# Splitting the FFN weights into bf16 pairs ahead of attention instead of inside the first FFN token block

## What is computed

```python
x = layernorm(x + attn(x, Wq, Wkv_down, Wk_up, Wv_up, Wo))      # 8 heads of 256, kv latent of 64
x = layernorm(x + ffn(x, W1, b1, W2, b2, scale))
# ffn, with S = 2048, D = 1024, H = 4096; W1 [H, D], W2 [D, H]
h = x @ W1.T + scale * (x @ m1.T) + b1       # m1, m2: rank-4 matrices made from a few tokens of x
h = gelu(h)                                  # exact gelu
out = h @ W2.T + scale * (h @ m2.T) + b2
```

## Time and profile before

| | us |
|---|---|
| two timed executions | 4051.82 and 4417.59 (median 4234.71) |
| the profiled execution, time | 4072.83 |
| the profiled execution, span of its slowest core | 4071.2 |
| spans of the 8 cores in it | 4036.4 to 4071.2 |
| FFN token block 0 / 1 (from L915 to the next L915) | 870.7 / 448.4 |

### The profile page before, as it was taken

The page is one execution under the profiler, slowest core; times in us unless marked ns, Lnnn a source line. Parts: engine busy times, 40 slices in busy tenths (PEclk is TensorE's granted clock), DMA queues, the critical chain, the costliest instruction groups (busy, mean ns, idle before and its releaser), DMA issues.

```text
span 4071.2 us, 32532 instructions; the slowest of 8 cores (4036.4 to 4071.2 us)
## 1 busy us (share of the span) xinstructions
PE 3140.4 (77%) x10424; PEld 1208.2 (30%) x10610; DVE 743.4 (18%) x1123; ACT 506.0 (12%) x729; POOL 547.4 (13%) x1144
## 2 busy tenths in 40 slices
PE   3647769889889789626666566569998899978997
PEld 1512223323323233202222122213443334423442
DVE  1112221121121121131111000014201331023201
ACT  0000014234234134100000000001000110001000
POOL 0000000000000000016664555510000000000000
PEclk8578879999999999857778777789998899989998
DMA  3130000010010010026554445433233232323232
GB/s 111 62 109 0 0 27 6 4 43 6 4 44 6 3 46 6 7 75 115 105 114 77 88 94 100 95 79 96 66 98 100 76 86 72 96 63 88 66 97 64
DMA packets 474216, 253.89 MB, mean 62 GB/s; under 512 B 125170, under 2 KB 452850, under 8 KB 473026
## 3 DMA queue, kind: packets, MB, share of 16 engines
q1 hardware_dynamic: 315938, 177.63, 15.9%
q0 software_dynamic: 79776, 32.20, 5.7%
q10 hardware_dynamic: 78336, 41.98, 3.5%
HBM read 177.49 MB, written 50.33 MB: 56 GB/s over the span
## 4 chain that ended last, share of the span: by engine, by line
PE 63%; DMA 10%; POOL 10%; DVE 9%; issue 4%; ACT 2%; SPq 1%; DVEq 0%; POOLq 0%; ACTq 0%
PE psU L592 11%; DMA whl<-w2f 5%; PE ps L337 4%; PE psY L624 3%; DMA whl<-w1f 3%; PE ps L562 3%; POOL whl L751 3%; POOL whl L743 3%; PE ps L565 3%; PE ps L558 2%; POOL whl L789 2%; PE ps L1065 2%; PE ps L1070 2%; PE ps L1075 2%; PE psY L962 2%
## 5 line engine op out<-in xcount | busy, mean ns | idle before, releaser
L592 PE MATMUL psU<-et,kvtok 128*65 128x512 f32 x1024 | 523.1, 598 | 2.6
L578 ACT ACTIVATE et<-ps,Ubias 128x512 f32<-128x512 f32 x512 | 351.7, 687 | 643.9 <-PE psU L592 431.8
L995 ACT ACTIVATE hgf<-htmp,b1s 128x512 f32<-128x512 f32 x128 | 92.3, 721 | 1738.5 <-DVE htmp L989 1685.9
L1065 PE MATMUL psY<-hphi,whl 128*128 128x512 bf16 x504 | 209.7, 416 | 80.0 <-POOL whl L797 79.0
L1065 PE MATMUL ps<-hphi,whl 128*128 128x512 bf16 x500 | 207.1, 414 | 79.0 <-POOL whl L797 78.1
L962 PE MATMUL psY<-z1s,whl 128*128 128x512 bf16 x505 | 212.8, 421 | 61.1 <-POOL whl L751 49.1
L962 PE MATMUL ps<-z1s,whl 128*128 128x512 bf16 x496 | 202.9, 409 | 67.3 <-POOL whl L751 65.7
L967 PE MATMUL psY<-z1s,whl 128*128 128x512 bf16 x499 | 211.0, 423 | 10.2 <-POOL whl L751 5.9
L1070 PE MATMUL psY<-hplo,whl 128*128 128x512 bf16 x500 | 208.0, 416 | 11.2 <-POOL whl L797 10.6
L443 DVE RECIPROCAL rcp<-psU 1x512 f32<-1x512 f32 x32 | 107.4, 3355 | 573.3 <-PE psU L592 573.3
L1070 PE MATMUL ps<-hplo,whl 128*128 128x512 bf16 x504 | 209.2, 415 | 3.1 <-POOL whl L797 2.2
(11 more groups left out here) (172 smaller groups left out, 3146.9 us busy)
## 6 DMA issues: line engine op xcount, KB each, us to landing
whl<-w1sd SPq DMA_DIRECT2D x768, 64.0 KB, 1.9
whl<-w2sd SPq DMA_DIRECT2D x768, 64.0 KB, 1.9
w1f<-w1p SPq DMA_DIRECT2D x256, 64.0 KB, 3.5
w1sd<-whl ACTq DMA_DIRECT2D x256, 64.0 KB, 3.6
w2f<-w2p SPq DMA_DIRECT2D x256, 64.0 KB, 2.9
w2sd<-whl ACTq DMA_DIRECT2D x256, 64.0 KB, 3.0
xTs<-xT SPq DMA_DIRECT2D x8, 1024.0 KB
wst<-wq SPq DMA_DIRECT2D x16, 512.0 KB, 5.4
```

The lines of the kernel that those rows point to most:

```text
L578: P.op("scalar", lambda e, kc=kc, par=par, h=h: e.activation(out=et[:, par * 512:(par + 1) * 512], in_=psA[par][:], func=AF.Exp, bias=Ubia ...
L592: P.op("tensor", lambda e, kc=kc, par=par, h=h: e.matmul(psU[h % 2][:], kvtok[:, kc * 65:(kc + 1) * 65], et[:, par * 512:(par + 1) * 512], ...
L1065: P.op("tensor", lambda e, d=d, k=k, s4w=s4w, hc=hc, st=st: e.matmul(psP[d % 4][:], whl2[:, s4w * 1024 + k * 256: s4w * 1024 + k * 256 + 128],
```

## The change

The splitting leaves tb = 0. A new `plan_split_block()` handles the next of 96 blocks (W1's 32, then W2's 64) with two buffers of its own, wspf (float32) and wspb (split), which live until the end of attention: ScalarE issues the loads, GpSimd the casts and the subtractions, ScalarE the stores into w1sd and w2sd. Three blocks are planned after each of the 8 heads of the query folding, three after each of the 8 heads of the output folding, three after each of the 16 query tiles; that makes 96, all planned ahead of the U8 transfers of L369 in GpSimd's list. `plan_w1` and `plan_w2` in all token blocks are what tb >= 1 had: SP loads from w1sd and w2sd, four blocks ahead. They wait for all stores (SPL_T). The buffers w1f and w2f and the stores of tb = 0 go.

```diff
+        sSLD = [sems["sW2C0"], sems["sW2C1"]]
+        sSCA = [sems["sW1C0"], sems["sW1C1"]]
+        sSST = [sems["sST0"], sems["sST1"]]
+        split_blocks = ([("w1", hc) for hc in range(HCN)]
+                        + [("w2", gi) for gi in range(64)])
+        spl = {"i": 0, "sub": {}, "st": {}}
+
+        def plan_split_block():
+            if spl["i"] >= len(split_blocks):
+                return
+            kind, idx = split_blocks[spl["i"]]
+            sl = spl["i"] % 2
+            spl["i"] += 1
+            if kind == "w1":
+                nch = DC
+                src_ap = lambda c, idx=idx: w1p[idx, c * 128:(c + 1) * 128, :]
+                dst_ap = lambda c, idx=idx: w1sd[idx, c * 128:(c + 1) * 128, :]
+            else:
+                d, g = divmod(idx, 8)
+                nch = 4
+                src_ap = lambda c, d=d, g=g: w2p[d, (g * 4 + c) * 128:(g * 4 + c + 1) * 128, :]
+                dst_ap = lambda c, d=d, g=g: w2sd[d, (g * 4 + c) * 128:(g * 4 + c + 1) * 128, :]
+            for c in range(nch):
+                P.op("scalar", lambda e, c=c, sl=sl, src_ap=src_ap: e.dma_start(
+                    out=wspf[:, sl * 1024 + c * 128: sl * 1024 + (c + 1) * 128],
+                    in_=src_ap(c)),
+                    waits=[(cG, spl["sub"].get(sl, 0))], inc=sSLD[sl], inc_k=16)
+            vL = sSLD[sl].n
+            for c in range(nch):
+                P.op("gpsimd", lambda e, c=c, sl=sl: e.dma_start(
+                    out=wspb[:, sl * 2048 + c * 256: sl * 2048 + c * 256 + 128],
+                    in_=wspf[:, sl * 1024 + c * 128: sl * 1024 + (c + 1) * 128]),
+                    waits=[(sSLD[sl], vL), (sSST[sl], spl["st"].get(sl, 0))],
+                    inc=sSCA[sl], inc_k=16)
+            vC = sSCA[sl].n
+            for c in range(nch):
+                P.op("gpsimd", lambda e, c=c, sl=sl: e.tensor_sub(
+                    wspb[:, sl * 2048 + c * 256 + 128: sl * 2048 + (c + 1) * 256],
+                    wspf[:, sl * 1024 + c * 128: sl * 1024 + (c + 1) * 128],
+                    wspb[:, sl * 2048 + c * 256: sl * 2048 + c * 256 + 128]),
+                    waits=[(sSCA[sl], vC)], inc=cG)
+            spl["sub"][sl] = cG.n
+            cGv = cG.n
+            for c in range(nch):
+                P.op("scalar", lambda e, c=c, sl=sl, dst_ap=dst_ap: e.dma_start(
+                    out=dst_ap(c),
+                    in_=wspb[:, sl * 2048 + c * 256: sl * 2048 + (c + 1) * 256]),
+                    waits=[(cG, cGv)], inc=sSST[sl], inc_k=16)
+            spl["st"][sl] = sSST[sl].n
...
@@ after each head of the query folding, and of the output folding
+            for _ in range(3):
+                plan_split_block()
...
@@ after each of the 16 query tiles, then ahead of the U8 transfers
+                for _ in range(3):
+                    plan_split_block()
+        while spl["i"] < len(split_blocks):
+            plan_split_block()
+        SPL_T = [(sSST[0], sSST[0].n), (sSST[1], sSST[1].n)]
...
@@ plan_w1 (plan_w2 likewise); the float32 loads, casts, subtractions and stores are gone
+            for c in range(DC):
+                P.op("sync", lambda e, hc=hc, c=c, s4=s4: e.dma_start(
+                    out=whl1[:, s4 * DC * 256 + c * 256: s4 * DC * 256 + (c + 1) * 256],
+                    in_=w1sd[hc, c * 128:(c + 1) * 128, :]),
+                    waits=[(cT, w1_free[s4])] + SPL_T,
+                    inc=sW1[s4], inc_k=16)
...
-                    wwt = ((cG, cG_w1[tb * HCN + hc]) if tb == 0
-                           else (sW1[s4], dS_w1[(tb, hc)]))
-                    ww = [wwt, (cV, cV_z1s), (cV, cV_ubc)]
+                    ww = [(sW1[s4], dS_w1[(tb, hc)]), (cV, cV_z1s), (cV, cV_ubc)]
```

More of the change, by code:

```diff
@@ L149, in build_nc @@
     qth_t = es_kv.enter_context(nc.sbuf_tensor("qth_t", [128, 4 * T], BF16, side="right"))
+    wspf = es_kv.enter_context(nc.sbuf_tensor("wspf", [128, 2 * 1024], F32, side="right"))
+    wspb = es_kv.enter_context(nc.sbuf_tensor("wspb", [128, 2 * 2048], BF16, side="right"))
     qtl_t = es_kv.enter_context(nc.sbuf_tensor("qtl_t", [128, 4 * T], BF16, side="right"))
@@ L723, in plan_w1 @@
         def plan_w1(tb, hc):
-            s = hc % 3
             s4 = hc % 4
[L726 to L734, removed]
@@ L735, in plan_w1 @@
-            for c in range(DC):
[L736 to L766, removed]
+            for c in range(DC):
+                P.op("sync", lambda e, hc=hc, c=c, s4=s4: e.dma_start(
[3 more added lines that the diff above has]
+                    inc=sW1[s4], inc_k=16)
@@ L768, in plan_w2 @@
+            dS_w1[(tb, hc)] = sW1[s4].n
         def plan_w2(tb, d, g):
             gi = d * 8 + g
-            s = gi % 3
             s4 = gi % 4
[L772 to L780, removed]
@@ L781, in plan_w2 @@
-            for k in range(4):
[L782 to L813, removed]
+            for k in range(4):
+                P.op("sync", lambda e, d=d, g=g, k=k, s4=s4: e.dma_start(
+                    out=whl2[:, s4 * 1024 + k * 256: s4 * 1024 + (k + 1) * 256],
+                    in_=w2sd[d, (g * 4 + k) * 128:(g * 4 + k + 1) * 128, :]),
+                    waits=[(cT, w2_free[s4])] + SPL_T,
+                    inc=sW2[s4], inc_k=16)
@@ L931, in build_nc @@
             dS_u4_prev = dS_u4
[L933 to L936, removed]
+            for pf in range(4):
                 plan_w1(tb, pf)
@@ L979, in build_nc @@
                 w1_free[s4] = cT.n
[L980 to L984, removed]
+                if hc + 4 < HCN:
+                    plan_w1(tb, hc + 4)
                 if hc == 2 and pending_ln2[0] is not None:
@@ L1047, in build_nc @@
             cV_r2 = [0] * DC
-            for pf in range(3 if tb == 0 else 4):
+            for pf in range(4):
                 plan_w2(tb, 0, pf)
@@ L1053, in build_nc @@
                         hc = g * 4 + k
-                        ww = [(cG, cG_w2[tb * 64 + d * 8 + g]) if tb == 0
-                              else (sW2[(d * 8 + g) % 4], dS_w2[(tb, d, g)])]
+                        ww = [(sW2[(d * 8 + g) % 4], dS_w2[(tb, d, g)])]
                         if g == 0 and k == 0:
@@ L1081, in build_nc @@
                     w2_free[(d * 8 + g) % 4] = cT.n
-                    if tb == 0:
-                        plan_w2_store(tb, d, g)
                     sidx = d * 8 + g
-                    adv2 = 3 if tb == 0 else 4
-                    if sidx + adv2 <= 63:
-                        nd, ng = divmod(sidx + adv2, 8)
+                    if sidx + 4 <= 63:
+                        nd, ng = divmod(sidx + 4, 8)
                         plan_w2(tb, nd, ng)
```

3 lines of the change are left out of this document (1 added, 2 removed).

## The result

The change makes the kernel slower: 4506.8 us median of eleven timed executions, and a ratio of 1.104 to the kernel before (95% interval 1.099 to 1.110). I had forecast 4359 us, 7.0% above the profiled execution of before and 2.9% above the median I was shown. The sign and the mechanism held, the size did not: between the two profiles the span grew by 454 us (4071.2 to 4525.5) where I had reckoned 286.

What follows compares the result with a forecast made beforehand. TensorE bounds most of the kernel, GpSimd's splitting tb = 0; after the change a serial splitting chain delays attention. 4071.2 - 454 + 740 = 4357 us of span, plus 1.6 gives 4359 us; range 4230 to 4700.

Steps and rivals of the forecast that it cites:

- The sign and the mechanism: Whole kernel: slower, 0.93, because splitting ahead of attention runs as a serial chain that delays the U8 transfers by 740 us.
- What is removed: 454 us: First FFN token block (tb = 0): without splitting it takes 416 us instead of 870.7, saving 454 us.
- The serial chain: Splitting before attention: ScalarE's in-order queue puts load(i+1) behind store(i), so blocks do not overlap; chance 0.80 at near-alone prices.
- What hides under it: Setup before attention: TensorE's whole setup work hides under the chain, and attention after U8 is as before.
- The length of the chain: 1258 us: Splitting before attention: 32 w1 blocks of 17.9 us and 64 w2 blocks of 10.7 us, U8 at 1274 us.
- my low bound: Chain with issues, landings and handoffs at their least and no delay from x: chain 1101 us, time 4187 us.
- The first rival, crowded prices: Chain: issues, load landings and cast waits cost what they did in crowded tb = 0; time 4695 us, chance 0.13.
- The third rival, GpSimd alone: Chain: loads run ahead of the stores' waits, so blocks cost GpSimd's part only; 3739 to about 3910 us, chance 0.03.
- The rule on issue times: Chain: by the skill's rule issues would drop out and the change's sign turn; the forecast instead charged 0.45 us an issue.

Runs made afterwards that it cites:

- the reordered kernel: The changed kernel with ScalarE issuing loads of block i+1 ahead of the stores of block i: span 3932.8 us, 0.969 of the kernel before.

## Why the prediction was right and where it was wrong

- **What is removed: 454 us.** Right. 456.0 measured (870.7 - 414.7). Reading token block 1 and taking out its layer norm gave the price of token block 0 within 2 us.
- **The serial chain.** Right, and shown: the same instructions with loads ahead end at 846.6 instead of 1439.4 us.
- **What hides under it.** Right. U8 to FFN is unchanged (+1.3 us), and the output folding's waits of 518 us cost nothing.
- **The length of the chain: 1258 us.** Wrong, and the failed step: U8 came at 1439.4, not 1274, 165 us later. The first block, whose loads run beside those of x, ended at 44.6 us instead of 33.9 (1 + 15 + 17.9, in which I had charged it eight store issues that nothing calls for), +11. From one block's last subtraction to the next's, the other 31 w1 blocks took 20.0 us on average instead of 17.9, +66, and the 64 w2 blocks 12.1 instead of 10.7, +89.
- **Which term.** On core 3, averaged over the blocks: hardly GpSimd's own: subtractions as reckoned, casts 4.4 and 2.2 us on average against 4.25 and 2.15, the cast wait 157.9 / 96 = 1.64 us against my 1.6. The issues somewhat: 7.4 us (w1) and 3.3 us (w2) against 6.75 and 3.15, 32 us in all. Mostly it is the time from the last load's issue to the first cast: 1.9 + 0.1 = 2.0 us by my sum, on average 3.0 (w1) and 3.4 (w2) measured, 122 us in all. Two errors made it. I took the handoff to GpSimd as 0.1 us from rows in which GpSimd hands over; into a DMA that GpSimd issues it is 0.60, which is 48 us over the chain. And I took 1.9 us to land, from SP's loads in the earlier trace rows; here the last load of a block landed after 2.4 us (w1) and 2.8 us (w2) on average, 74 us in all. More than half of these 74 belong to cores 2 and 3 alone, as the time is that of the slowest core: on the other six the w2 loads landed after 2.1 to 2.2 us on average, a w2 block took 11.3 to 11.5 us, and the chain ended 93 to 125 us late instead of 165. What slowed the loads of two cores is open; the stores ahead of them did not do it, as the other six had them too. Why the rest landed later than SP's is open as well.
- **The size of the change.** I reckoned from the profiled 4072.8 us and compared with a median of two times, 4051.8 and 4417.6 us. Against that median my 4359 was a change of 2.9%, against the profiled execution 7.0%; the measured one is 10.4%. A slip beside it: the parts of my low bound add up to 15.7 and 9.5 us a block, not 15.6 and 9.4, which moves its 4187 up by 7 us and changes nothing.
- **The first rival, crowded prices.** Its 4695 us was too much: the cast wait kept a median of 1.4 us, the alone price. The issues did come at about its price (0.44 to 0.48 us each, medians), and the loads went part of the way to its 3.5 and 2.9.
- **The third rival, GpSimd alone.** Rightly refused for this code, but it describes what the reordered kernel does: its 3739 to 3910 us against a time of 3934.4, a little above the upper figure.
- **The rule on issue times.** The Trainium skill, DMA: Bandwidth & Descriptors, section "Issuing engines are not separate DMA queues", calls the time to start a DMA usually small relative to the DMA itself. Here one issue of a 64 KB piece was 0.44 to 0.48 us, about a fifth of its landing (2.2 us). In a chain that waits for all of them the issues add up: sixteen in a row made 7.5 of a w1 block's 20.0 us, and fewer, larger DMAs took 258 us off.

## What to carry to other kernels

Two buffers overlap nothing if one in-order queue holds the store of a block ahead of the load of the next: write out each queue's list before counting on a pipeline. Work moved "under" another stage still binds whatever stands behind it in the same queue, here four tiny transfers that open attention. Price the start of what waits as a term of its own, from a row in which the same kind of instruction starts after a wait. And before a step of the slowest core's trace is explained, look at the same step on the other cores: what only two cores of eight show does not come from the order of the code alone.

## What the runs showed of the hardware

- A DMA that GpSimd issues after a wait starts 0.60 us after the signal (median of 95 blocks), a copy of GpSimd's 0.18 us. The trace of before had it already, in rows I did not read: the 16 BT transfers start 0.55 to 0.62 us after VectorE's copy ended, and the last qpm operation of VectorE ended 0.59 us before U8 started at 534.22:

```profile
533.48 0.15 DVE L364 TENSOR_TENSOR qpm<-qpm,tmp 2x1 f32<-2x1 f32 x1
```

- A 128x128 copy from float32 to bf16 on GpSimd took 0.24 us (eight in 1.95); as a DMA cast the same tile held GpSimd for 0.53 us and landed 1.8 us after its issue (medians).
- One 512 KB load landed in 5.4 us; eight of 64 KB needed 5.5 us from the first issue to the last landing (medians of the slowest cores). For the chain that is nearly the same.
- The last 64 KB load of a block landed after 2.0 to 2.5 us behind stores issued ahead of them (w1 blocks on eight cores, w2 blocks on six), and after 2.0 to 2.4 us with no store ahead; with stores from SP starting at the same moment it was 2.5 to 3.1 us. Two cores of eight had 3.0 and 2.9 us in the w2 blocks of one execution; no run here shows why.
